# A top-ten attention layer: gathering the chosen rows as wide tiles on column strips and turning them later

## What is computed

```python
scores = einsum('bnd,d->bn', base_hidden, score_w[0]) + score_b[0]
_, topk_idx = top_k(scores, 10)
sparse_hidden = take_along_axis(base_hidden, topk_idx[:, :, None], axis=1)   # (16, 10, 256)
q = heads(sparse_hidden @ Wq.T + bq); k = heads(context @ Wk.T + bk); v = heads(context @ Wv.T + bv)
attn = softmax(q @ k.T / sqrt(16));  o = attn @ v                              # 16 heads of 16
return base_hidden.at[arange(B)[:, None], topk_idx].set(o @ out_w.T + out_b)
```

## Time and profile before

| | us |
|---|---|
| median of 3 runs (1336.75 to 1339.53) | 1338.59 |
| the profiled execution, its own time | 1333.26 |
| its span from first to last instruction | 1331.3 |
| PE busy in it | 1221.5 (92%) |
| DVE, ACT, POOL busy | 726.0, 610.6, 428.4 |

### The profile page before, as it was taken

How to read it: one execution, slowest core, us unless ns; L and a number is a source line. 1 busy time by engine, 2 the same in 40 slices (tenths; PEclk the granted TensorE clock), 3 DMA queues, 4 the chain that set the end, 5 groups by cost and what they waited for, 6 DMA issues and landing times.

```text
span 1331.3 us, 36286 instructions
## 1 busy us (share of the span) xinstructions
PE 1221.5 (92%) x14818; PEld 1024.4 (77%) x14818; DVE 726.0 (55%) x1656; ACT 610.6 (46%) x1464; POOL 428.4 (32%) x545
## 2 busy tenths in 40 slices
PE   4899999966899999999988969999999999999986
PEld 2567666655689989989766859999999999876655
DVE  5688787777322000000376457757667567537775
ACT  2455555522545445444322225545445445435552
POOL 3224446164222222226200033424424434232200
PEclk9999999978999999999977879999999999999997
DMA  9000000000589999999620010100100101000000
GB/s 317 3 2 2 2 2 18 10 18 25 175 292 331 336 323 353 353 341 324 210 74 2 2 41 22 41 22 22 42 21 26 38 21 36 8 1 5 23 18 25
DMA packets 91573, 130.73 MB, mean 98 GB/s; under 512 B 13393, under 2 KB 74065, under 8 KB 91281
## 3 DMA queue, kind: packets, MB, share of 16 engines
q1 hardware_dynamic: 85360, 117.11, 26.5%
q0 software_dynamic: 4768, 10.26, 2.1%
q10 hardware_dynamic: 1280, 1.04, 0.2%
HBM read 116.82 MB, written 11.57 MB: 96 GB/s over the span
## 4 chain that ended last, share of the span: by engine, by line
PE 76%; DVE 10%; DMA 4%; issue 3%; ACT 3%; POOL 2%; SPq 1%; ACTq 0%; another core or an unknown queue 0%; DVEq 0%; POOLq 0%
PE scores L1778 9%; PE bank L1788 9%; PE bank L2336 8%; PE scores L1472 7%; PE bank L1472 6%; PE bank L491 5%; PE scores L508 4%; DVE reg L880 4%; PE scores L518 3%; PE bank L540 3%; PE bank L500 3%; PE scores L2326 3%; PE scores L2312 3%; PE bank L529 2%; PE scores L1980 2%
## 5 line engine op out<-in xcount | busy, mean ns | idle before, releaser
L1823 ACT ACTIVATE w_ca<-scores,fc1b 128x128 f32<-128x128 f32 x312 | 114.2, 367 | 144.7 <-PE scores L1778 123.9
L1778 PEld LDWEIGHTS scores<-reg 128*128 128x128 f32 x1248 | 148.3, 195 | 9.3 <-DMA reg<-in_fc 5.0
L1778 PE MATMUL scores<-reg 128*128 128x128 f32 x1248 | 149.2, 279 | 6.3 <-DMA reg<-in_fc 4.2
L1857 DVE TENSOR_TENSOR reg<-bank,reg 128x256 f32<-128x256 f32 x39 | 16.6, 424 | 245.6 <-PE bank L1788 230.2
L2406 ACT ACTIVATE reg<-reg,mx 128x128 f32<-128x128 f32 x256 | 99.3, 389 | 106.0 <-DVE mx L2557 106.0
L880 DVE TENSOR_REDUCE reg<-scores 128x8 f32<-128x1024 f32 x96 | 113.0, 1219 | 61.6 <-PE scores L508 61.5
L1788 PE MATMUL bank<-reg,w_ca 128*128 128x256 f32 x624 | 141.1, 379 | 0.3 <-DVE small L1848 0.3
L1788 PEld LDWEIGHTS bank<-reg,w_ca 128*128 128x128 f32 x624 | 115.6, 190 | 14.5 <-DVE small L1848 0.3
L2336 PE MATMUL bank<-reg,w_ca 128*128 128x256 f32 x496 | 115.0, 385 | 0.0
L774 ACT ACTIVATE reg<-scores 128x1024 f32<-128x1024 f32 x96 | 92.9, 1021 | 44.3 <-PE scores L518 40.2
L2336 PEld LDWEIGHTS bank<-reg,w_ca 128*128 128x128 f32 x496 | 91.8, 190 | 15.6 <-issue 2.6
(11 more groups left out here) (308 smaller groups left out, 2261.7 us busy)
## 6 DMA issues: line engine op xcount, KB each, us to landing
reg<-in_fc SPq DMA_DIRECT2D x78, 1024.0 KB, 7.7
w_sa<-grouped_values SPq DMA_DIRECT2D x64, 128.0 KB, 2.6
reg<-expert_out SPq DMA_DIRECT2D x16, 256.0 KB, 3.0
xres<-in_x SPq DMA_DIRECT2D x4, 512.0 KB, 10.9
ctxr<-in_ctx SPq DMA_DIRECT2D x1, 2048.0 KB, 15.5
w_l<-in_w_l SPq DMA_DIRECT2D x2, 1024.0 KB, 13.4
routed_rows<-reg SPq DMA_DIRECT2D x8, 256.0 KB
grouped_values<-reg SPq DMA_DIRECT2D x16, 128.0 KB, 1.7
```

What stands on the lines that cost most here:

```text
L1778: ins = nc.tensor.matmul(S[n % 4][:, 0:P], up_w8[j % 2][:, c, f * P:(f + 1) * P], xbT[:, j % 2, c, :], start=(c == 0), stop=(c == C - 1))
L1823: nc.scalar.activation(h1[:, j % 2, f, :], S[n % 4][:, 0:P], ACT.Gelu, bias=fc1b[:, bass.ds(e * FC + f, 1)]).then_inc(M["fc1_free"], 1)
```

## The change

Before, the gathering makes the chosen rows in turned form at once: for each of the four batches and each half of the values, a 128 x 128 block of `xres` is the stationary operand and the 32 columns of `gat` are streamed (eight matmuls, each 128x32). Now `gat`'s 32 columns are the stationary operand and all 256 values of `xres` are streamed, so a batch's result is 32 places by 256 values and lands on its own 32 partitions of the bank: four matmuls, each on its own strip of 32 columns of the array. The result has places on the partitions, so it is copied out by ACT, turned by PE in two transpositions (`turn_chosen`), and copied out by ACT again over the same memory (`turned_copy`). For g = 0 the turn stands right behind; for the others it stands behind the products of the group before. The two-bank list gets a further entry, `xr`, for the gathering, and `xg` now names the turn.

```diff
-        in_turn = [("bias", 0)] + [(n, 2) for n in KV] + [("row", 0), ("xg", 0), ("q", 0)]
+        in_turn = [("bias", 0)] + [(n, 2) for n in KV] + [("row", 0), ("xr", 0), ("xg", 0), ("q", 0)]
         for g in range(G):
             if g + 1 < G:
-                in_turn += [("row", g + 1), ("xg", g + 1)]
+                in_turn += [("row", g + 1), ("xr", g + 1)]
             in_turn += {1: [("hc0", 3), ("hc1", 3)], 2: [("v0", 3), ("v1", 3)]}.get(g, [])
             if g + 1 < G:
-                in_turn += [("q", g + 1)]
+                in_turn += [("xg", g + 1), ("q", g + 1)]
...
             def chosen_rows(g):
+                bank = tok_claim(pe, ("xr", g))
+                pe.wait_ge(M["tok_gat_ok"], g + 1)
+                for j in range(GB):
+                    nc.tensor.matmul(bank[mine(j), 0:D], gat[:, j, :], xres[:, g * GB + j, :], start=True, stop=True)
+                nc.tensor.transpose(bank[:, D:D + P], gat[:, :, :].rearrange("p j r -> p (j r)"), ident[:])\
+                    .then_inc(tok_done(("xr", g)), 1)
+
+            def turn_chosen(g):
                 bank = tok_claim(pe, ("xg", g))
-                pe.wait_ge(M["tok_gat_ok"], g + 1)
+                tok_await_moved(pe, ("xr", g))
                 for c in range(C):
-                    for j in range(GB):
-                        nc.tensor.matmul(bank[:, c * P + j * R:c * P + (j + 1) * R], xres[:, g * GB + j, c * P:(c + 1) * P],
-                                         gat[:, j, :], start=True, stop=True)
-                nc.tensor.transpose(bank[:, C * P:C * P + P], gat[:, :, :].rearrange("p j r -> p (j r)"), ident[:])\
-                    .then_inc(tok_done(("xg", g)), 1)
+                    ins = nc.tensor.transpose(bank[:, c * P:(c + 1) * P], chosen_T[:, g % 2, c * P:(c + 1) * P], ident[:])
+                ins.then_inc(tok_done(("xg", g)), 1)
...
             keep_warm(3)
             chosen_rows(0)
+            turn_chosen(0)
             queries(0)
...
                 if g + 1 < G:
+                    turn_chosen(g + 1)
                     queries(g + 1)
...
             def chosen_copy(g):
-                bank = tok_await(act, ("xg", g))
+                bank = tok_await(act, ("xr", g))
                 if g >= 2:
                     act.wait_ge(M["tok_put_full"], g - 1)
-                nc.scalar.activation(chosen_T[:, g % 2, :], bank[:, 0:3 * P], ACT.Copy).then_inc(tok_moved(("xg", g)), 1)
+                nc.scalar.activation(chosen_T[:, g % 2, :], bank[:, 0:3 * P], ACT.Copy).then_inc(tok_moved(("xr", g)), 1)
+
+            def turned_copy(g):
+                bank = tok_await(act, ("xg", g))
+                nc.scalar.activation(chosen_T[:, g % 2, 0:D], bank[:, 0:D], ACT.Copy).then_inc(tok_moved(("xg", g)), 1)
...
             chosen_copy(0)
+            turned_copy(0)
             queries(0)
...
+                if g + 1 < G:
+                    turned_copy(g + 1)
                 even_heads(g)
...
                 if g > 0:
-                    tok_await(dve, ("xg", g - 1))
+                    tok_await(dve, ("xr", g - 1))
```

## The result

The changed kernel takes 1332.19 us in the median of 8 runs, the kernel before beside it 1339.06. The ratio is 0.9944, with a 95% interval of 0.9923 to 0.9965: about 7 us faster. Repeated twice in other comparisons it came out at 0.9952 (0.9935 to 0.9969) and 0.9956 (0.9926 to 0.9986). The forecast was 2.3 us faster, with a range whose lower end, 1332.5, the median passes by 0.3. The sign and most of the steps held; the two terms that hang on when the clock returns did not.

A forecast was written before the change was run, and what follows sets the result against it. The prediction took PE as the bound, mostly at half clock in this stretch; -0.3 - 0.45 - 0.5 - 1.0 = -2.25 us, carried to the median of 1338.59, gave 1336.3 us, range 1332.5 to 1339.8.

The forecast's parts named there:

- the price of the wide gathering: Four 256-column matmuls per group, priced from the put_back row: 0.71 us at full and 1.24 at half clock.
- the products at g = 0 held by the exponentials: Loop step g = 0: products wait for ACT's exponentials, start 1.64 us earlier, about 2.1 behind the turned scores' end.
- the round trip: Between the gathering's copy and the queries: two transpositions, ACT's second copy, hand-offs; 0.93 us at full, 1.21 at half clock.
- group 0: First group, gathering at full clock, round trip uncovered: minus 1.23 plus 0.93, -0.3 us; from -0.5 to +0.8.
- step g = 0: First loop step: products 1.64 us earlier, less 1.21 added ahead of the queries; taken as -0.45 us.
- the round trip covered by DVE at g = 2: Last loop step: the added 0.93 us lies beside DVE's divide; DVE still releases the output rows.
- The 0.23 us a drain, five times: Five more tile-shape changes, each draining PE by a Trainium skill rule, would give back 1.15 us; not in the sum.
- step g = 1: Second loop step: products 1.95 us earlier, -0.75 with the round trip, about 0.25 lost to the clock; taken as -0.5.
- step g = 2: Last loop step: values products start 2.07 us earlier at half clock, clock returning at the same moment; -1.0 us.
- One of the prediction's own signs of being wrong: Stated as wrong if half clock in the steps lasts over 2 us longer or shorter than before.
- the clock returns earlier: Rival, three loop steps: full clock returns sooner as dense work moves up; sum -4 us, about 1334.5; chance 0.25.
- the clock returns later: Rival, steps g = 0 and 1: the gap before the queries delays full clock; +1.8 to +3 us, 1341; chance 0.09.

## Why the prediction was wrong

Right, by its own steps: the price of the wide gathering (0.71 and 1.24 taken, 0.64 and 1.08 measured; the four strips do overlap); the products at g = 0 held by the exponentials (2.1 us behind the turned scores, as written); the round trip (0.93 at full and 1.21 at half clock taken; in group 0, from the end of the first copy to the queries, 673.51 to 674.62, it is 1.11 with its first hand-off, and at g = 0, at half clock, 1.25 from the first transposition, 691.67, to the queries, 692.92); group 0 (-0.3 forecast, -0.44 in the mean of the profiles, and -0.21 where the clock is full on both sides, 5.48 against 5.27); step g = 0 (-0.45 forecast, -0.51 measured); the round trip covered by DVE at g = 2. The 0.23 us a drain, five times, that the prediction set beside its sum do not show: the gathering is shorter than put_back's row, and group 0 at full clock comes within 0.1 of the sum without them, where its two changes of shape would have cost 0.46.

Wrong in size: the terms of step g = 1 and step g = 2. The prediction put -0.5 and -1.0, the profiles say -1.82 and -2.66 from the gathering to the scores, or -1.5 and -1.6 if the turned scores ahead are counted too. At g = 2 the failing sentence is "If the clock returns at the same moment, 2.07 earlier at half clock is worth 1.0". The clock's return was treated as fixed in time, though the work ahead of it moved. For a fall equally far ahead of the gathering it came 3.4 us sooner, and the values products kept their length instead of growing by a microsecond. The 2.07 was too small too: the values products start 2.40 earlier, since the gathering is shorter than its price and the turn of `gat` was added in full where it overlaps. At g = 1 the product start came 1.98 earlier as forecast (-1.95), but then 0.25 was taken off for a later clock and the round trip was charged at half clock in front of queries at half clock. In all five profiles of the changed kernel the clock was full by the queries (1.13 us, before 1.76 in the first profile), and in four of them already during the products. One of the prediction's own signs of being wrong is met: from the gathering to the scores the half clock is shorter by 3.9 us at g = 1 (8.1 to 4.2 in the mean) and by 2.9 at g = 2 (6.8 to 3.9).

These two terms are 1.6 to 3.0 us too small, a third to two thirds of the 4.6 by which the gain was missed. The rival "the clock returns earlier" named the cause, with 1.4 us for step g = 2 and the rest to a sum of -4, and gave it a quarter of the chance. Its sum is the 4.0 that the layer gains in the profiles. The rival "the clock returns later" was right in part, for the longer half clock at g = 0.

Two more things went into the miss. The price of the last loop step was read off a single profile, and the half clock in the layer differs between profiles of one kernel by up to 18 us (30.6 and 48.9). And the range ended 0.3 us short of the median. What remains open: the timed gain is 6 to 7 us and the layer in the profiles only 4.0 us shorter; the whole span of the nine profiled executions is only 1.1 us shorter in the mean (1332.6 and 1331.5). The three are compatible, since four and five profiles, with a scatter of the layer of some 2.6 and 1.3 us and a larger one of the span, tell the difference of the means to about 3 and 5; no profile shows a gain elsewhere, so 2 to 3 us of the timed gain are not located. Why narrow matmuls keep the clock down, and whether it is they or the start of dense work that decides, was not separated: few narrow ones and a dense long gathering each helped.

## What to carry to other kernels

Where a stretch runs at half clock until dense work comes, a microsecond taken out ahead of that dense work can be worth more than the half microsecond that a fixed return of the clock would leave: do not hold the moment of the return fixed when you move what leads to it. The gain comes in jumps, and a single profile can mislead, so look at several profiles of the same kernel before pricing a step. In a kernel like this one, take the short form of a small selection (the mask stationary, the wide rows streamed, one strip per batch) and put the turn that it then needs behind work that is long enough to cover the other engine's copy; put right behind the selection, it gave most of the gain back.

## What the hardware showed unexpectedly

Four 128-row matmuls of 256 columns on four column strips into one bank took 0.64 us at full clock and 1.08 at half, against 1.89 and 3.62 for the same four on one strip. Filling short idle gaps with matmuls that nobody reads did raise the clock once where it was meant to (queries 1.05 instead of 2.05 us), but in no comparison the speed (0.9970 and 0.9971 against 0.9952 and 0.9956). Heavier filling among narrow matmuls held the clock nearly full and cost 26 to 27 us. In the top-ten layer of all nineteen profiles a stretch of half clock lasted 3.4, 6.8, 10.2 or 13.7 us, and nothing between. Such a stretch can begin while PE is busy: in the run on one strip it began at 738.56, when the turned scores (128 records of 32 columns) had run for 3.1 us without a gap.
